# GpSimd multiplies half of the tile picks by the token number; the softmax's last part, one weight load and a stream of filler matmuls change places around it

## The reference

```python
w = weights[conditions]                       # 32 of 200 matrices, 64 x 64
xf = einsum('bct,bcd->bdt', x, w)             # x is 32 x 64 x 512: 2048 tokens of 512
gate = softmax(xf @ Wr.T)                     # 8 experts
top2 = top_k(gate, 2)
rank = running count of the expert's picks; keep = rank <= 640
g, u = silu(xf @ Wg[e].T), xf @ Wu[e].T       # inner width 352
y = sum over the two picks of gate * ((g * u) @ Wd[e].T)
return x + y
```

## Time and profile before

| | |
|---|---|
| time, median of 3 runs | 289.1 us (289.03 to 290.47) |
| the profiled execution's own time | 288.85 us |
| its span from the first to the last instruction | 287.0 us |
| granted TensorE clock, mean over the span | 0.982 |
| busy: PE, DVE, ACT, POOL | 275.1, 126.4, 127.9, 164.3 us |
| first matmul of the main loop | 43.7 us from the span's start |

### The profile page before, as it was taken

How to read it: one execution, slowest core, us unless ns; L and a number is a source line. 1 busy time by engine, 2 the same in 40 slices (tenths; PEclk the granted TensorE clock), 3 DMA queues, 4 the chain that set the end, 5 groups by cost and what they waited for, 6 DMA issues and landing times.

```text
span 287.0 us, 4871 instructions
## 1 busy us (share of the span) xinstructions
PE 275.1 (96%) x1735; PEld 237.9 (83%) x1736; DVE 126.4 (44%) x256; ACT 127.9 (45%) x213; POOL 164.3 (57%) x150
## 2 busy tenths in 40 slices
PE   8999799999999999999999999999999999999990
PEld 4663339989999999999999999999999999999970
DVE  1658945433353345444353443354335544442210
ACT  2347914444444455444544444444445545533320
POOL 5790068332387575776445558675758568573232
PEclk9999869999999999999999999999999999999997
DMA  6995989999389787858676659787977765644536
GB/s 207 374 315 207 380 203 366 303 393 371 97 108 242 167 198 183 177 138 167 138 186 138 154 138 224 134 169 197 181 163 197 187 136 81 127 80 50 69 39 73
DMA packets 28913, 53.50 MB, mean 186 GB/s; under 512 B 7200, under 2 KB 7328, under 8 KB 28896
## 3 DMA queue, kind: packets, MB, share of 16 engines
q0 software_dynamic: 10576, 21.67, 41.6%
q1 hardware_dynamic: 18320, 31.60, 32.6%
HBM read 32.74 MB, written 20.25 MB: 185 GB/s over the span
## 4 chain that ended last, share of the span: by engine, by line
PE 93%; DVE 2%; ACT 1%; issue 1%; POOLq 1%; POOL 1%
PE bank L997 47%; PE bank L1018 25%; PE bank L979 5%; PE bank L1029 4%; PE bank L854 3%; PE bank L965 2%; PE bank L866 2%; PE bank L916 2%; PE bank L877 1%; PE bank L910 1%; PE bank L959 1%; POOLq L83 1%; POOL out L498 1%; PE bank L899 1%; ACT tiles L525 0%
## 5 line engine op out<-in xcount | busy, mean ns | idle before, releaser
L498 POOL DMA_INDIRECT out<-tiles,dst_row x40 | 64.9, 1623 | 34.0 <-DMA out<-tiles,dst_row 13.2
L997 PE MATMUL bank<-whi,xhi 128*128 128x352 f32 x280 | 70.7, 333 | 0.8 <-ACT xhi L571 0.8
L486 POOL DMA_INDIRECT gate_g<-gates_dram,src_row x40 | 41.9, 1047 | 51.5 <-ACT tiles L588 44.8
L997 PE MATMUL bank<-wlo,xhi 128*128 128x352 f32 x280 | 67.7, 323 | 0.0
L806 DVE TENSOR_TENSOR xlo<-bank,xhi 128x512 fp32r<-128x512 f32 x35 | 24.2, 692 | 77.2 <-ACT xhi L571 77.2
L476 POOL DMA_INDIRECT tiles<-xf_dram,src_row x40 | 41.0, 1025 | 27.7 <-DVE dst_row L797 15.8
L997 PE MATMUL bank<-whi,xlo 128*128 128x352 f32 x280 | 56.6, 323 | 0.0
L997 PEld LDWEIGHTS bank<-whi,xhi 128*128 128x128 f32 x280 | 48.0, 189 | 4.2 <-issue 1.4
L997 PEld LDWEIGHTS bank<-wlo,xhi 128*128 128x128 f32 x280 | 48.8, 188 | 0.0
L571 ACT ACTIVATE xhi<-bank 128x512 fp32r<-128x512 f32 x35 | 20.9, 597 | 58.7 <-PE bank L979 58.7
L997 PEld LDWEIGHTS bank<-whi,xlo 128*128 128x128 f32 x280 | 47.0, 189 | 0.0
(11 more groups left out here) (99 smaller groups left out, 237.8 us busy)
## 6 DMA issues: line engine op xcount, KB each, us to landing
raw<-wgu SPq DMA_DIRECT2D x32, 352.0 KB, 4.4
x_sb<-x SPq DMA_DIRECT2D x8, 512.0 KB, 7.8
raw<-wd SPq DMA_DIRECT2D x8, 512.0 KB
out<-x_sb SPq DMA_DIRECT2D x4, 1024.0 KB, 9.0
xf_dram<-tiles SPq DMA_DIRECT2D x7, 512.0 KB, 3.3
raw<-wd SPq DMA_DIRECT2D x8, 192.0 KB
out<-x_sb SPq DMA_DIRECT2D x1, 1280.0 KB, 15.2
tiles<-xf_dram,src_row POOLq DMA_INDIRECT x40, 4.5
```

Source lines behind the costliest of these rows:

```text
L486: nc.gpsimd.indirect_dma_start(out=gate_g[:, n % TPE, :], out_offset=None, in_=gates_dram[:, :], in_offset=bass.IndirectOffsetOnAxis(ap=sr ...
L498: nc.gpsimd.indirect_dma_start(out=out[:, :], in_=y_sb[:, n % TPE, :], in_offset=None, out_offset=bass.IndirectOffsetOnAxis(ap=dst_row[:, ...
L997: last = nc.tensor.matmul(ps[:, 0:I], left[:, b, c], right[:, half, o:o + I], start=(k == 0 and left is xhi and right is whi), stop=(k == ...
```

## The change

Five things change.

1. The comparison L761 is made in two halves of the 32 groups, the second half first, each signalling `where_ok`. GpSimd multiplies the second half by the token number (new, signals `second_ok`), VectorE the first half (signals `what_ok` as before). TensorE waits for `second_ok` before the 17th of its 32 pick matmuls.
2. `subtract`, `exps` and `gates` are no longer cut at tile 10. One subtraction (tiles 14, 15) stays ahead of `one_hot(1)`, the other (tiles 0 to 13) comes behind it; the exponential moves behind all of ScalarE's `xf_copy` and its first `w_high`; `gates` moves behind the lists and all of VectorE's `w0_low` for the gate and up weights. The write of the gates moves behind SyncE's wait for the first gathered tile.
3. The down weights of expert 0 are loaded right behind its other weights.
4. TensorE's order: of `condition(2)` only half its matmuls (`qs=(0,)`) stay ahead of `turn(NM - 1)`; the other half comes behind `logits(3)`. Only `condition(4)` is then left ahead of the ranks, where there were two pairs, so five pairs follow the ranks instead of four.
5. Of the 18 filler matmuls behind the picks 14 stay, and 8 new ones run ahead of the picks (`AHEAD_OF_PICKS`).

```diff
-            for u in range(KH):
+            for u in range(NU):
                 load_unit(0, u)
...
-            sp.wait_ge(gates_ok, 2)
+            sp.wait_ge(xg_in[0], 16)
+            sp.wait_ge(gates_ok, 1)
             sp.dma_start(gates_dram.rearrange("(j p) e -> p j e", p=P),
                          gate[:, :, :]).then_inc(gates_out, 16)
-            load_unit(0, KH)
-
-            sp.wait_ge(xg_in[0], 16)
...
+            pool.wait_ge(consts, CONSTS)
+            pool.wait_ge(where_ok, 1)
+            second = slice(HALF_A, A)
+            nc.gpsimd.tensor_tensor(pick_t[:, :, second], pick_t[:, :, second],
+                                    number[:, :, second], ALU.mult).then_inc(second_ok, 1)
+
             pool.wait_ge(lists_ok, 1)
...
-            exps(0)
...
             for u in range(W0_EARLY):
                 w_high(u, 0, 0)
-            for n in range(XR, XR + 2):
-                xf_copy(n, n - XR)
-            exps(1)
...
+            act.wait_ge(sub_ok, 2)
+            nc.scalar.activation(ex[:, :, :], lg[:, :, :], ACT.Exp).then_inc(ex_ok, 1)
             for u in range(W0_EARLY, KH):
                 w_high(u, 0, 0)
...
-            subtract(0, GATED)
+            dve.wait_ge(consts, RANKS)
             xrT_copy(NM - 1)
             xr_sum(NM - 2)
-            gates(0)
+            one_hot(0)
             xr_sum(NM - 1)
-            dve.wait_ge(consts, RANKS)
-            one_hot(0)
             top_two(2)
             top_two(3)
-            subtract(GATED, LG[3][0] * 2)
             subtract(LG[3][0] * 2, TT)
             one_hot(1)
-            gates(1)
+            subtract(0, LG[3][0] * 2)
...
-            link(nc.vector.tensor_tensor(pick_t[:, :, :], iota_t[:, :, :],
-                                         slot_tp[:, 0, :].unsqueeze(1).broadcast_to(wide),
-                                         ALU.is_equal))
-            nc.vector.tensor_tensor(pick_t[:, :, :], pick_t[:, :, :], number[:, :, :],
+            for h in (1, 0):
+                part_a = slice(h * HALF_A, (h + 1) * HALF_A)
+                nc.vector.tensor_tensor(pick_t[:, :, part_a], iota_t[:, :, part_a],
+                                        slot_tp[:, 0, part_a].unsqueeze(1)
+                                        .broadcast_to([P, NT, HALF_A]),
+                                        ALU.is_equal).then_inc(where_ok, 1)
+            dve.wait_ge(where_ok, 2)
+            first = slice(0, HALF_A)
+            nc.vector.tensor_tensor(pick_t[:, :, first], pick_t[:, :, first], number[:, :, first],
                                     ALU.mult).then_inc(what_ok, 1)
...
             for u in range(W0_EARLY, KH):
                 w0_low(u)
+            gates()
...
-            condition(2)
+            condition(2, (0,))
             turn(NM - 1)
             logits(2)
             logits(3)
-            after = EARLY_PAIRS * 2 + BEFORE_RANKS
-            for j in range(EARLY_PAIRS * 2, after, 2):
-                condition(j)
+            condition(2, (1,))
+            condition(4)
...
-            for j in range(after, TT, 2):
+            for j in range(6, TT, 2):
                 condition(j)
 
+            def keep_warm(n, ps):
+
+                for _ in range(n):
+                    nc.tensor.matmul(ps, iota_q[:, 0:P // AQ, :].rearrange("p q a -> p (q a)"),
+                                     iota_q[:, 0:H // AQ, :].rearrange("p q a -> p (q a)"),
+                                     start=True, stop=True)
+
             pe.wait_ge(consts, CONSTS)
+            pe.wait_ge(sub_ok, 2)
+            keep_warm(AHEAD_OF_PICKS, bank[4])
             pe.wait_ge(what_ok, 1)
             for a in range(A):
+                if a == HALF_A:
+                    pe.wait_ge(second_ok, 1)
...
-            for _ in range(KEEP_WARM):
-                nc.tensor.matmul(ps_hT[:, :], iota_q[:, 0:P // AQ, :]
...
+            keep_warm(KEEP_WARM, ps_hT)
```

More of the change, by code:

```diff
@@ L21 @@
 A = TOP * TT
+HALF_A = A // 2
 Q = 32
@@ L39 @@
 AQ = 8
-BEFORE_RANKS = 4
 EARLY_OUT = 0
@@ L44 @@
 LG = ((0, 3), (3, 5), (5, 7), (7, NM))
-GATED = 2 * LG[1][1]
-EARLY_PAIRS = 2
 WARM_UP = 10
-KEEP_WARM = 18
+AHEAD_OF_PICKS = 8
+KEEP_WARM = 14
 PASS = 2 * TPE
@@ L218, in build @@
         what_ok = sem("what_ok")
+        where_ok = sem("where_ok")
+        second_ok = sem("second_ok")
         pick_ok = sem("pick_ok")
@@ L541, in w_high @@
                 nc.scalar.activation(whi[:, half, a:b], raw[:, a:b], ACT.Copy).then_inc(whi_ok, 1)
-            def exps(h):
-                act.wait_ge(sub_ok, (1, 3)[h])
-                js = (slice(0, GATED), slice(GATED, TT))[h]
-                nc.scalar.activation(ex[:, js, :], lg[:, js, :], ACT.Exp).then_inc(ex_ok, 1)
-            for n in range(2):
+            for n in range(XR):
                 xf_copy(n, n)
-            exps(0)
-            for n in range(2, XR):
-                xf_copy(n, n)
+            with act.Fori(1, TT // XR) as i:
+                for s in range(XR):
+                    xf_copy(i * XR + s, s)
             for u in range(W0_EARLY):
                 w_high(u, 0, 0)
-            for n in range(XR, XR + 2):
-                xf_copy(n, n - XR)
-            exps(1)
-            for n in range(XR + 2, 2 * XR):
-                xf_copy(n, n - XR)
-            with act.Fori(2, TT // XR) as i:
-                for s in range(XR):
-                    xf_copy(i * XR + s, s)
+            act.wait_ge(sub_ok, 2)
+            nc.scalar.activation(ex[:, :, :], lg[:, :, :], ACT.Exp).then_inc(ex_ok, 1)
             for u in range(W0_EARLY, KH):
@@ L901, in logits, with condition @@
                 last.then_inc(lg_ps, 1)
-            def condition(j):
+            def condition(j, qs=(0, 1)):
                 if j >= XR:
                     pe.wait_ge(xf_ok, j - XR + 2)
-                for q in (0, 1):
+                for q in qs:
                     for n in (j, j + 1):
@@ L911, in condition @@
                                                 x_sb[rows, n, :], start=True, stop=True)
-                last.then_inc(xf_ps, 2)
+                if 1 in qs:
+                    last.then_inc(xf_ps, 2)
             pe.wait_ge(warm_clear, 1)
```

17 lines of the change are left out of this document (6 added, 11 removed).

## The result

The changed kernel takes 293.74 us (median of 4 executions, 293.27 to 294.28) against 289.06 us of the kernel before (288.93 to 290.47) on the same chip. The ratio is 1.0151, 95% interval 1.0119 to 1.0184. The prediction was 288.7 us with a range of 287.6 to 290.4.

The account below looks back on a forecast made before the run. TensorE's fixed matmul round was taken as the bound, so only the loop's start counted: 288.85 us less 0.4 gave 288.45, and 0.25 for the median gave 288.7, range 287.6 to 290.4.

Parts of the forecast that it names:

- one assumption behind it: TensorE's main loop: nothing in the change touches its round of matmuls, about 6.7 us a tile.
- Ranks, scan, last copy: Ahead of the picks: ranks and scan 0.65 us earlier, last copy of xf ending at about 33.95, 0.7 later.
- The last write: Last write of xf, ahead of the first gather: landing at 37.25 us, ends 36.7 and 37.4.
- The lists: Behind the picks: src_row at 36.95 to 37.1 us, lists 0.85 us later than before.
- The split: Pick multiplication shared by VectorE and GpSimd: saves 0.35 us on VectorE, GpSimd's half taking 1.5 us.
- The rival that GpSimd holds VectorE: Pick multiplication: VectorE stands for GpSimd's whole instruction; at 2.6 us 0.7 slower, 289.8 us; chance 0.09.
- deciding point of 1.9 us: Fillers ahead of the picks: VectorE could lose 1.9 us before TensorE notices.
- the slower rival: First tiles: the clock falls after TensorE's idleness; 3.5 us of low clock costs 1.75, 290.4 us; chance 0.15.
- Late gates: First scaling: ScalarE stands waiting for gates, with the third tile's high part behind it; 289.7 us; chance 0.08.
- empty queues: First gather: meets empty queues, lands in 3.1 us from 38.0, gain 1.0, 288.1 us; chance 0.20.

Follow-up runs that it names:

- d_fill28: The changed kernel with 28 instead of 14 fillers behind the picks: 290.74 us, ratio 1.0053 to the kernel before.
- b_order: The kernel before with the new TensorE order alone (half of condition(2) behind logits(3), five pairs behind the ranks): 290.77 us, ratio 1.0118.
- again_after: The changed kernel, unchanged, run again on a second chip: 292.13 us, ratio 1.0139 to the kernel before.
- d_order_wd_fill: The changed kernel with TensorE's order of before, down weights behind the writes of xf and 23 fillers behind the picks: 290.03 us, ratio 1.0011.
- b_fillers: The kernel before with the new fillers alone, 8 ahead of the picks and 14 instead of 18 behind: 291.62 us over ten executions, ratio 1.0079.

## Why the prediction was wrong

The sum had four steps ahead of the loop and one assumption behind it.

**Ranks, scan, last copy: right in direction, sizes off.** The scan came at 27.32 and 27.46 where 27.05 was forecast (d_fill28: 26.91). The last copy ended at 34.26, forecast 33.95, for that reason: 6.94 us behind the scan, forecast 6.90.

**The last write: the term that was mis-sized.** "coming later it waits a little less. I put its landing at 36.7 + 0.55 = 37.25; ends 36.7 (all hidden by the queue) and 37.4." It landed at 39.08, 1.7 us above the upper end. Of the 2.35 us that it is later than before, 1.0 is the later copy and 1.35 the longer write (4.80 for 3.45). The step that failed is "The down weights go into SP's queue at 17.9 us, behind unit 3; the first write of xf is issued at 23 and the queue has room between. Cost 0." The room was there (share 0.09 ahead of the first write) and the weights took all of it; the first write then took 4.1 us, where the kernel before's took 2.8 (23.02 to 25.78).

What lasts from there is not a backlog of all sixteen DMA engines. Between the first and the second write they are nearly idle, 20 GB/s in the changed kernel and nothing in b_order (new order, late weights):

```profile
26.00:27.00 1.00, 0.66 (x5) 0.22 (x3) 0.78 (x4) 1.00 (x3) 0.00 (x0) 1.00 0.05 20
```

```profile
26.00:27.00 1.00, 0.72 (x4) 0.00 (x0) 0.93 (x9) 1.00 (x3) 0.00 (x0) 1.00 0.00 0
```

What lasts is one engine that is late. The DMA view of 27.6 to 29.4 us in the changed kernel has an instruction packet beside xf:

```profile
q1 hardware_dynamic: 347, 0.68, 97.8%
q8 instruction: 1, 0.02, 5.8%
```

A share of 5.8% of sixteen engines over 1.8 us is 1.67 us of one engine. The trace's packet records tell whose time it was: fifteen engines begin the second write at 27.57 to 27.72 us and the sixteenth at 29.32, while the instruction packet runs from 27.68 to 29.33. From 28 us on xf keeps the engines full (share 0.79 to 1.06 in each microsecond up to 36), and the late engine does not catch up. Fifteen are through with the last write at 37.0, the one at 38.7. The DMA view of 36.9 to 39.1 us shows it (forty slices of GB/s, packets, queues with their share of 16 engines):

```profile
GB/s 75 298 37 37 0 37 37 0 37 37 0 37 37 0 37 37 37 0 37 37 0 37 37 0 37 37 0 37 37 0 37 37 0 0 0 0 0 0 0 0
DMA packets 33, 0.06 MB, mean 29 GB/s; under 512 B 9, under 2 KB 9, under 8 KB 32
## 3 DMA queue, kind: packets, MB, share of 16 engines
q1 hardware_dynamic: 32, 0.05, 5.7%
q8 instruction: 1, 0.02, 3.6%
```

One packet of xf follows another at an even pace (37 GB/s or 0 in a slice). The instruction packet in this window (3.6% of 2.2 us, 1.27 us of one engine, from 37.0) does not slow them, so it is the earlier one that counts. The Trainium skill, Runtime: NRT & Kernel Launch, section "Instruction fetch mechanics", says that each engine's instruction memory is refilled through DMA in blocks of 16 KiB; the 0.02 MB packet agrees in size.

All twenty traces fit this. In the three with the long last write (changed, again_after, d_fill28) the instruction packet takes 1.66, 1.58 and 1.47 us, comes 4.8 to 4.9 us after the first write's issue and 0.9 to 1.0 after the second's, and the last engine ends 1.8, 1.6 and 1.5 us behind the others. The records do not number the engines: that it is the one that stood behind the packet is concluded from these times, and no run takes the packet away. In the other seventeen the packet comes 2.4 to 2.5 us after the first write's issue, and the last engine is at most 0.24 us behind. With the new order that is 1.5 us ahead of the second write; with the old one it is 0.4 to 0.5 behind its issue, and the engines then have gaps in which the late one catches up (share 0.35 from 27 to 28 us in the kernel before). So the early weights lengthen the first write, and the packet comes 2.4 us later, into the stretch without gaps. Why it moves with them no run shows. The new order with late weights, b_order, has 3.59 us, so the order alone does not do it. An undisturbed run of the early weights with the old order was not made, so how much of the 1.35 us needs both is open.

**The lists: right. The split: wrong in sign, and hidden.** Picks from 34.68 to 37.23 at full clock (forecast 34.4 to 36.9), `src_row` at 37.27 (forecast 36.95 to 37.1, so 0.2 late), GpSimd's multiplication 31.34 to 32.84, 1.50 us (forecast 1.5 from 31.3). The rival that GpSimd holds VectorE happened as described and stayed under its deciding point of 1.9 us: VectorE lost about 1.1. The rule of the Trainium skill on the shared port that the prediction cites, SBUF — State Buffer, section "SBUF: two separate sides", agrees with the trace: 1.57 us for an instruction that fits in some 0.45, ended just behind GpSimd's. But the step "saves 0.35" was wrong in sign: it is 0.82 later. I had given the lock as a rival where the diff itself made it the likely case: GpSimd starts on the first `where_ok` and VectorE on the second, which come 0.4 us apart, and both then read `pick_t` and `number`. It cost nothing only because eight fillers stood ahead of the picks.

**The clock: the assumption that decided.** The prediction wrote the slower rival down with its mechanism, "TensorE is now idle from 40.1 to 41.95 and again for about 0.8 ahead of the loop", and gave it 0.15 with a price of 1.75 us. Measured: idle from 40.26 to 43.89, the lower level for 6.8 us by the windows, and 2.06 us more between the first two turnings (5.46 for 3.40; 1.5 more in again_after). By the ratios with and without the longer fillers it is 0.86% of 289, 2.5 us, by the medians 1.8. The error has two parts. "Against: fillers on both sides of the picks" counted fillers and not the time that they fill: 14 at full clock are 3.0 us and had to cover 39.83 + 3.92 - 37.23 = 6.5 us. And the same row that I read as "1.2 us is all that shorter or faster fillers can bring" says the reverse when turned round: the slow fillers of before outlasted the gather, and their low clock was over (0.96 at 41 us) when the first tile came. Making them fast and fewer moved the low stretch from work that nobody reads to work that counts.

**Late gates, empty queues.** The gates' write took 4.7 us and their gathers began at 48.77, 4.5 later than before and 2.8 later than forecast; no wait of the scaling over 0.2 us shows in the undisturbed traces, and the kernel that keeps the late gates is at 1.0011. The gather took 3.9 us from 39.83 in the changed kernel and 3.4 in again_after and d_fill28, against 3.7 forecast: the queues are empty as that rival said, and it is not quicker by much.

So of 1.39 to 1.51%, 0.6 to 0.9 is the clock under the first tile (d_fill28), and the other 0.4 to 0.5 goes when TensorE's order and the early weights are taken back (d_order_wd_fill, 1.0011). How these two share it is not settled: the copy's 1.0 us belongs to the order, the write's 1.35 to the late DMA engine, which appeared only with the early weights.

## What to carry to other kernels

Size filler matmuls in time, against the latest arrival of what they wait for, and at the clock that they will have. Fewer or faster ones leave a hole, and in four of six traces here the clock then fell under the first real work. A load moved into an idle stretch just ahead of a burst of writes is not free: here it made the first write longer and shifted what came behind it. A transfer is done only when the last of its DMA engines is, so look at the tail of the last one, packet by packet, before you name a cause. Handing half of an elementwise instruction to GpSimd brought nothing here, since VectorE ran its own half at the same time and took 1.57 us for it.

## What the runs showed of the hardware that was not expected

- One GpSimd multiplication of 128 x 640 f16 values took 1.50 or 1.51 us in every trace, and beside it VectorE's instruction of the same size took 1.57 us where some 0.45 is its own.
- A write of 256 KB took from 3.2 to 4.8 us. In the long ones a single DMA engine was 1.5 to 1.8 us behind, and moved the last part alone at 37 GB/s or 0 in a slice.
- An instruction packet of 16 KiB kept one DMA engine from its share of a write for 1.66 us (changed kernel, 27.68 to 29.33 us); nine microseconds later the last engine was still 1.8 us behind.
- With the same kernel the granted clock fell further in some executions than in others (b_fillers: mean 0.980 to 0.994, 292.95 to 288.11 us).
